# Context stage of a perceiver layer: two products written as 64-column halves, and another order of transfers on SyncE

## The chip, the core and the metric

The kernel runs on one core of a Trainium2 chip. The metric is the device time of one execution in microseconds (us), as the median of several. All data are f32 unless said otherwise.

## What is computed

The reference adds three blocks to x (64 sequences of 64 tokens, 256 features). Only the first concerns this change:

```python
v = jnp.einsum('bsd,hd->bsh', visual_features, Wv) + bv     # of layernorm(x), 64 tokens per sequence
t = jnp.einsum('bsd,hd->bsh', text_features, Wt) + bt       # of ctx_768, 256 rows of 192 features per sequence
dots = jnp.einsum('bih,bjh->bij', v, t)
vn, tn = jnp.linalg.norm(v, axis=-1), jnp.linalg.norm(t, axis=-1)
return dots / jnp.maximum(vn[:, :, None] * tn[:, None, :], EPS)   # added to x
```

The second block is a self-attention with 16 heads, the third a mixture of 14 experts of which each token takes one.

## The kernel before

There are three stages: context (the block above), attention, experts. The context stage goes through 16 pairs of sequences (NB = 16; one pair is 128 tokens twice, that is two tiles of tokens). All engines run the same list of pairs, each with an order written out by hand, and wait for each other on counting semaphores. TensorE's step for pair i holds, in this order:

- t's first pass (lines 1303 and 1306): 128 of the 192 context features, two products with 512 moving columns each, into two PSUM banks (`t_bank(p, 0)` and `t_bank(p, 1)`). The stationary operand is `wt_s`, 128 columns wide.
- the values v (line 1324, from the fifth pair on; the first four, `TURNED = 4`, use line 1327 on turned tiles): two products with 256 moving columns, stationary `wvc_s`, 128 columns wide, moving `xT_s`.
- t's second pass (line 1352): the other 64 features, two products on 64 rows of the array each.
- for the pair before: v's squared norms (line 1293), t's squared norms (line 1363, two products on 64 columns of the array), and the dots (line 1367, four products on 64 columns, 256 moving columns each).

The step for the 15th pair also holds some small products for the router (lines 1376, 1341, 1344), the one for the 16th a transposition for attention (line 1282).

What follows for a pair: VectorE multiplies norms (line 724), ScalarE takes logarithm and exponential (1103, 1105), VectorE makes the cosines (755), GpSimd adds them to the tokens (528), VectorE takes statistics of the sum (709, 714). TensorE's line 1293 of the next pair waits for the cosines of this one (`cos_sbuf`). From the fifth pair on v is made of raw x: VectorE (line 696) adds the bias times each token's standard deviation to it, and for that it needs the deviations along the free axis on all partitions. They are made by GpSimd (`deviation`, lines 491 to 498, six pairs ahead, after its line 528), written to memory by SyncE (line 356) and read back as 128 copies into `std_b` (line 365, `spread_deviations`). After line 696 ScalarE squares v (1115) and evacuates t (1125, 1126) before it comes to line 1103 again.

SyncE asks for nearly all transfers from one queue, in order; a wait there holds up everything behind it. Its step i (`load_tokens`) waits for t's second pass of pair i-4, then asks for xT and the context of pair i (lines 344, 345; four buffers), spreads the deviations of pair i-2, asks for x of pair i+3 (i+2 in the first steps), and writes the deviations of pair i (`deviations`), for which it waits for GpSimd. In steps 8 to 13 two constants each follow. `std_b` has two buffers.

On GpSimd, VectorE, ScalarE and TensorE some of the middle steps stand in a hardware loop of four steps per turn (`run_steps`), which makes one turn (two on ScalarE).

Of the kernel before, what the change touches and what calls it, by code (L numbers as in the profile page):

```python
# [15 lines left out]
P = 128  # L16
B, S, D = 64, 64, 256
SC, DC, H = 256, 192, 128
# [5 lines left out]
NB = NT // 2  # L24
# [19 lines left out]
TURNED = 4  # L44
AHEAD = 6
LO, HI = 8, 28
RING, RLO, RHI = 8, 12, 28
# [78 lines left out]
def build(nc, x, xT, ctxT, wvT, wtT, xb, wqT, wkT, avT, woT, bq, bk, bv, bo, boc, woN, routerT, w1, w2, b1T, b2, out):  # L126
# [3 lines left out]
    with ctx:  # L130
# [3 lines left out]
        def sem(name):  # L134
            return ctx.enter_context(nc.semaphore(name))
# [58 lines left out]
        vT, vsq = (arena[:, 4096 + n * 2 * D:4096 + (n + 1) * 2 * D].rearrange("p (s j) -> p s j", s=2) for n in range(2))  # L194
        std_b = arena[:, 2048:2048 + 4 * P].rearrange("p (s j) -> p s j", s=2)
        wvc_s = arena[:, 2048 + 4 * P:2048 + 4 * P + KC * H].rearrange("p (c h) -> p c h", c=KC)
        pair_rstd, pair_rvar, pair_std = (arena[:, 3072 + n * NT:3072 + (n + 1) * NT] for n in range(3))
# [100 lines left out]
        ctx_in = [sem(f"ctx_in{n}") for n in range(4)]  # L298
        std_in = [sem(f"std_in{n}") for n in range(2)]
        std_out = [sem(f"std_out{n}") for n in range(2)]  # L300
        rec_out = [sem(f"rec_out{n}") for n in range(RING)]
# [23 lines left out]
        def _(sp):  # L325
# [9 lines left out]
            def load_tokens(i, k):  # L335
# [5 lines left out]
                else:  # L341
                    need(sp, s["t_psum"], i - 3)
                    if not isinstance(i, int) or i >= TURNED:
                        sp.dma_start(xT_s[:, k], xT[bass.ds(i, 1)].rearrange("o p j -> (o p) j")).then_inc(ctx_in[k], 16)
                    sp.dma_start(ctx_in_sb[:, k], ctxT[bass.ds(i, 1)].rearrange("o p j -> (o p) j"))\
                        .then_inc(ctx_in[k], 16)
                def turned(n):
                    return isinstance(n, int) and not TURNED <= n < NB
                if not turned(i - 2):
                    spread_deviations(i - 2, k % 2)  # L350
                for n in (i + 2,) if i < 4 else (i + 2, i + 3) if i == 4 else (i + 3,):
                    if n < NB:
                        load_x(n, n % 4)
                if not turned(i):
                    need(sp, s["a_std"], i - TURNED + 1)
                    sp.dma_start(deviations[bass.ds(i, 1)].rearrange("o p h -> (o p) h"), pair_std[:, bass.ds(i * 2, 2)])\
                        .then_inc(std_out[k % 2], 16)
                if 8 <= i < 8 + RESTS // 2:
                    for to, source in rest[2 * (i - 8):2 * (i - 7)]:
                        sp.dma_start(to, source).then_inc(s["consts_in"], 16)  # L360

            def spread_deviations(n, q):
                need(sp, std_out[q], arrivals(n - TURNED, q, 2, 16))
                need(sp, s["v_sbuf"], n - 1)
# [4 lines left out]
            for n in (NB - 2, NB - 1):  # L369
                spread_deviations(n, n % 2)  # L370

# [66 lines left out]
        def _(pool):  # L438
# [97 lines left out]
            def attention_step(i, k):  # L536
# [49 lines left out]
                return send  # L586
            run_steps(pool, context_step, -4, NB - 1, 6, 10)
            pool.wait_ge(s["consts_in"], 16 * RESTS)
# [47 lines left out]
        def _(dve):  # L636
# [13 lines left out]
            def context_step(j, k):  # L650
# [39 lines left out]
                if paired(v) and not (isinstance(v, int) and v < TURNED):  # L690
                    need(dve, s["v_psum"], v + 1)
                    need(dve, s["dots_psum"], v - 1)
                    need(dve, std_in[p], arrivals(v - TURNED, p, 2, 16))
                    if isinstance(v, int) and v == TURNED:
                        dve.wait_ge(s["first_made"], 6)
                    dve.scalar_tensor_tensor(vT[:, p, :].rearrange("f (h t) -> f h t", h=2),
                                             std_b[:, p, :].rearrange("f (t h) -> f h t", h=2), xbs_s[:, :],
                                             bank(p, 2 * P).rearrange("f (h t) -> f h t", h=2), ALU.mult, ALU.add)\
                        .then_inc(s["v_sbuf"], 1)
# [61 lines left out]
            def attention_step(i, k, parts=("tile", "ranked", "lcs", "sums", "late"), aside=()):  # L761
# [145 lines left out]
                if live(u):  # L907
                    need(dve, s["smax_ok"], u + 1)
                    need(dve, s["pT_psum"], u - 1)
                    if isinstance(u, int) and u == 0:  # L910
# [3 lines left out]
                        .then_inc(s["centred"], 1)  # L914
            run_steps(dve, context_step, -4, NB - 3, 6, 10)
            attention_step(-1, 3)
# [172 lines left out]
        def _(act):  # L1089
# [71 lines left out]
            def attention_step(i, k):  # L1161
# [39 lines left out]
                if live(u):  # L1201
                    spread_second_values((k - 1) % 2, (k - 1) % 4)
            run_steps(act, context_step, -1, NB, 4, 12)
            context_step(NB, NB)
# [66 lines left out]
        def _(pe):  # L1271
# [13 lines left out]
            def context_step(i, k):  # L1285
# [10 lines left out]
                if paired(t):  # L1296
# [5 lines left out]
                    need(pe, s["t_sbuf"], t - 1)  # L1302
                    pe.matmul(t_bank(p, 0), wt_s[:, 0, :], ctx_in_sb[:, k, 0:2 * SC], start=True, stop=False)
                    if isinstance(i, int) and i == 0:
                        pe.wait_ge(ctx_in[0], 16)
                    pe.matmul(t_bank(p, 1), wt_s[:, 0, :], ctx_in_sb[:, k, 2 * SC:4 * SC], start=True, stop=False)
                    if isinstance(i, int) and i == 0:
# [119 lines left out]
            def attention_step(i, k):  # L1427
# [84 lines left out]
            run_steps(pe, context_step, -1, NB, 8, 12)  # L1512
            pe.wait_ge(s["consts_made"], CONSTS)
# [164 lines left out]
```

## Time and profile before

| | us |
|---|---|
| median of 3 runs | 495.55 |
| lowest and highest run | 494.43, 496.55 |
| profiled execution | 494.51 |
| its span, first to last instruction | 492.7 |
| TensorE busy | 479.8 (97% of the span) |
| VectorE, ScalarE, GpSimd busy | 335.6, 331.6, 243.9 |

The profiled execution spends 1.81 us outside its span. The context stage fills the time to about 104 us, attention the next 235 us or so, the experts the rest; they overlap a little. Matmuls are pipelined, so their rows overlap: the time a product takes is read from one start to the next. An f32 product makes two MATMUL records, hence "x2" for one product, "x4" for two.

### The profile page before, as it was taken

The numbers are of one execution on the slowest core, as the hardware profiler recorded it, in microseconds if no ns is written. First come the engines' busy times: TensorE is split into PE (matmuls) and PEld (weight loads), VectorE is DVE, ScalarE is ACT, GpSimd is POOL, SyncE is SP. The second block draws the span as 40 slices with busy tenths as digits, with TensorE's granted clock in tenths as the row PEclk, the third lists the DMA queues.
The fourth block names the chain that finished last, engine by engine and source line by source line (L and its number), as shares of the span: only waits on it lengthen the run. The fifth ranks groups of instructions, "written<-read, shape, count | busy, mean of one in ns | idle before, by whom it ended". The sixth has DMA issues, their size and how long they took to land.

```text
span 492.7 us, 13958 instructions
## 1 busy us (share of the span) xinstructions
PE 479.8 (97%) x4290; PEld 384.0 (78%) x4291; DVE 335.6 (68%) x1021; ACT 331.6 (67%) x804; POOL 243.9 (50%) x428
## 2 busy tenths in 40 slices
PE   8999999999999999999999999998999999999996
PEld 6544444567888888888888888877898999999995
DVE  3577665657788989999898999998573333333332
ACT  2765666569988998898898889886553334333432
POOL 3468764344444456474655657472555333233333
PEclk9999999999999999999999999999999999999999
DMA  8989997500001223313322221227465876675631
GB/s 305 284 195 298 297 311 207 177 2 2 1 2 39 51 88 98 98 61 87 100 57 91 67 59 51 67 84 227 152 220 160 266 229 203 207 232 192 193 131 37
DMA packets 35025, 69.32 MB, mean 141 GB/s; under 512 B 6592, under 2 KB 21826, under 8 KB 34960
## 3 DMA queue, kind: packets, MB, share of 16 engines
q1 hardware_dynamic: 31168, 59.40, 40.3%
q0 software_dynamic: 3360, 8.84, 4.8%
q8 instruction: 34, 0.56, 0.5%
q10 hardware_dynamic: 432, 0.26, 0.2%
q14 instruction: 31, 0.25, 0.2%
HBM read 57.61 MB, written 11.35 MB: 140 GB/s over the span
## 4 chain that ended last, share of the span: by engine, by line
PE 65%; DVE 6%; issue 4%; ACT 3%; POOL 2%; POOLq 0%; ACTq 0%; DVEq 0%
PE psum L1532 13%; PE psum L1545 12%; PE psum L1459 9%; PE psum L1436 6%; PE psum L1423 6%; PE psum L1415 6%; PE psum L1383 5%; PE psum L1488 5%; PE psum L1282 5%; DVE arena L912 1%; POOL tok L528 1%; POOL out L614 1%; ACT arena L1145 0%; DVE smax L901 0%; ACT arena L1181 0%
## 5 line engine op out<-in xcount | busy, mean ns | idle before, releaser
L1532 PEld LDWEIGHTS psum<-arena,ring 128*128 128x128 f32 x608 | 73.5, 192 | 2.6 <-issue 0.6
L1532 PE MATMUL psum<-arena,ring 128*128 128x128 f32 x608 | 74.1, 275 | 0.5 <-issue 0.5
L1545 PE MATMUL psum<-w_s,arena 128*128 x304 | 71.9, 380 | 0.0
L1215 ACT ACTIVATE arena<-psum 128x256 f32<-128x256 f32 x38 | 14.6, 385 | 81.7 <-PE psum L1282 74.8
L1036 DVE SCALAR_TENSOR_TENSOR arena<-psum,slot_rec,arena 128x256 f32<-128x256 f32 x38 | 18.4, 484 | 69.3 <-PE psum L1545 69.0
L556 POOL TENSOR_TENSOR ov<-o_n,v_s 128x256 f32<-128x256 f32 x32 | 26.1, 817 | 77.8 <-DVE o_n L794 77.8
L1545 PEld LDWEIGHTS psum<-w_s,arena 128*128 128x128 f32 x304 | 55.0, 190 | 6.1
L1181 ACT ACTIVATE arena<-kT,head_mask 128x256 f32<-128x256 f32 x128 | 59.3, 531 | 0.0
L614 POOL DMA_INDIRECT out<-arena,token_of x38 | 38.8, 1022 | 19.0 <-POOL token_of L606 14.1
L901 DVE TENSOR_REDUCE smax<-psum 128x16 f32<-128x1024 f32 x32 | 39.2, 1224 | 12.6 <-PE psum L1436 12.6
L1145 ACT ACTIVATE arena<-arena 128x1024 f32<-128x1024 f32 x32 | 33.8, 1057 | 19.0 <-DVE arena L912 18.9
L1221 ACT ACTIVATE arena<-psum,b_s 128x128 f32<-128x128 f32 x152 | 43.3, 375 | 3.5 <-PE psum L1532 2.2
L552 POOL DMA_INDIRECT routed<-rec,pos x32 | 33.5, 1047 | 15.0 <-issue 6.5
L1415 PEld LDWEIGHTS psum<-arena 128*64 128x64 f32 x1024 | 32.4, 138 | 9.5 <-issue 8.3
L912 DVE TENSOR_TENSOR arena<-psum,smax 128x1024 f32<-128x1024 f32 x32 | 37.9, 1183 | 0.0
L606 POOL TENSOR_TENSOR token_of<-slot_rec,zero_u 128x1 uint32<-128x1 uint32 x38 | 9.1, 239 | 58.1 <-DVE arena L1036 58.0
L1436 PE MATMUL psum<-arena,qT 64*64 64x256 f32 x512 | 35.0, 389 | 1.6 <-DVE arena L912 1.6
L1415 PE MATMUL psum<-arena 128*64 128x34 f32 x1024 | 36.1, 225 | 0.4 <-ACT arena L1131 0.3
L1488 PE MATMUL psum<-av_s,xnT 128*128 128x270 f32 x128 | 34.7, 393 | 1.2 <-DVE logit L813 1.1
L1423 PE MATMUL psum<-wo_s,oT 128*128 128x270 f32 x128 | 35.2, 397 | 0.3 <-ACT oT L1141 0.3
L1459 PEld LDWEIGHTS psum<-xnT,wq_s 128*128 128x128 f32 x256 | 33.2, 191 | 2.2
L1459 PE MATMUL psum<-xnT,wk_s 128*128 128x128 f32 x256 | 34.2, 276 | 0.7 <-issue 0.7
(206 smaller groups left out, 1072.9 us busy)
## 6 DMA issues: line engine op xcount, KB each, us to landing
ring<-w SPq DMA_DIRECT2D x38, 512.0 KB
w_s<-ctxT SPq DMA_DIRECT2D x15, 768.0 KB, 8.5
w_s<-w SPq DMA_DIRECT2D x16, 448.0 KB, 3.4
slot_rec<-routed SPq DMA_DIRECT2D x38, 132.0 KB
tok<-x SPq DMA_DIRECT2D x16, 256.0 KB, 7.8
w_s<-xT SPq DMA_DIRECT2D x12, 256.0 KB, 6.8
routed<-pad_rec SPq DMA_DIRECT2D x1, 1980.0 KB, 8.6
tok<-b SPq DMA_DIRECT2D x14, 128.0 KB, 3.1
```

Of the source, the lines that this page charges most:

```text
L614: pool.indirect_dma_start(out=out, out_offset=bass.IndirectOffsetOnAxis(ap=token_of[:, q, :], axis=0), in_=yout[:, q, :], in_offset=None, ...
L901: dve.tensor_reduce(smax[:, :], s_ps, AX.X, ALU.max).then_inc(s["smax_ok"], 1)
L912: dve.tensor_tensor(prob[:, (k - 1) % 2, :].rearrange("p (h j) -> p h j", h=NH), s_ps, smax[:, :].unsqueeze(2).broadcast_to([P, NH, S]), A ...
L1181: last = act.activation(kd[:, p, :, :, g * S:(g + 1) * S], kT[:, p, :].rearrange("p (c b j) -> p c b j", c=KC, b=2), ACT.Copy, scale=head_ ...
L1221: last = act.activation(hidT[:, p, f * P:(f + 1) * P], hid_bank(p)[:, f * P:(f + 1) * P], ACT.Gelu, bias=b1_s[:, bass.ds(e * FC + f, 1)])
L1415: mm = pe.matmul(bank(7)[h, n * VW:(n + 1) * VW], probT[:, p, n * P + b * S:n * P + (b + 1) * S], vd[:, p, b, n, :], start=True, stop=True)
L1423: mm = pe.matmul(bank(6, DX), oT[:, q, d * P:(d + 1) * P], wo_s[:, d, :], start=d == 0, stop=d == KC - 1)
L1436: mm = pe.matmul(bank(g)[h, c * HG * S:(c + 1) * HG * S], qT[r, q, c * P + b * S:c * P + (b + 1) * S], kd[r, q, c, b, :], start=True, stop ...
L1459: mm = pe.matmul(bank(4)[:, at:at + P], weight[:, d, c * P:(c + 1) * P], xnT[:, p, d * P:(d + 1) * P], start=d == 0, stop=d == KC - 1)
L1488: mm = pe.matmul(bank(6, DX), xnT[:, p, d * P:(d + 1) * P], av_s[:, d, :], start=d == 0, stop=d == KC - 1)
L1532: mm = pe.matmul(hid_bank(p)[:, f * P:(f + 1) * P], w1_s[:, r, c * F + f * P:c * F + (f + 1) * P], xgT[:, p, c * P:(c + 1) * P], start=c = ...
L1545: mm = pe.matmul(bank(2 + q, D), hidT[:, q, f * P:(f + 1) * P], w2_s[:, bass.ds(e * (FC * D) + f * D, D)], start=f == 0, stop=f == FC - 1)
```

## The change

- t's first pass and the values are issued, from the fifth pair on, as two products each, one for either half of 64 output columns (64 PSUM partitions); the moving operand is the same for both.
- `std_b` has four buffers (`SPREAD = 4`) in place of two, with semaphores to match; `wvc_s` moves in the arena.
- SyncE asks for x before it spreads deviations, and from the sixth step for x of pair i+4 instead of i+3. From the ninth step it spreads pair i-1 instead of i-2, and writes the deviations of pair i+1 instead of i; the ninth step does two of each.
- The hardware loops of the context stage on the four engines are written out.

```diff
-        std_b = arena[:, 2048:2048 + 4 * P].rearrange("p (s j) -> p s j", s=2)
-        wvc_s = arena[:, 2048 + 4 * P:2048 + 4 * P + KC * H].rearrange("p (c h) -> p c h", c=KC)
+        std_b = arena[:, 2048:2048 + 8 * P].rearrange("p (s j) -> p s j", s=SPREAD)
+        wvc_s = arena[:, 3328:3328 + KC * H].rearrange("p (c h) -> p c h", c=KC)
...
-                def turned(n):
-                    return isinstance(n, int) and not TURNED <= n < NB
-                if not turned(i - 2):
-                    spread_deviations(i - 2, k % 2)
-                for n in (i + 2,) if i < 4 else (i + 2, i + 3) if i == 4 else (i + 3,):
+                for n in (i + 2,) if i < 4 else (i + 2, i + 3) if i == 4 else (i + 3, i + 4) if i == 5 else (i + 4,):
                     if n < NB:
                         load_x(n, n % 4)
-                if not turned(i):
-                    need(sp, s["a_std"], i - TURNED + 1)
-                    sp.dma_start(deviations[bass.ds(i, 1)].rearrange("o p h -> (o p) h"), pair_std[:, bass.ds(i * 2, 2)])\
-                        .then_inc(std_out[k % 2], 16)
+                first = TURNED + 4
+                if i >= TURNED + 2:
+                    for n in (i - 2,) if i < first else (i - 2, i - 1) if i == first else (i - 1,):
+                        spread_deviations(n)
+                if i >= TURNED:
+                    for n in (i,) if i < first else (i, i + 1) if i == first else (i + 1,):
+                        if n < NB:
+                            write_deviations(n)
...
-            def spread_deviations(n, q):
-                need(sp, std_out[q], arrivals(n - TURNED, q, 2, 16))
-                need(sp, s["v_sbuf"], n - 1)
+            def write_deviations(n):
+                sp.wait_ge(s["a_std"], n - TURNED + 1)
...
+            def spread_deviations(n):
+                q = n % SPREAD
+                sp.wait_ge(std_out[q], arrivals(n - TURNED, q, SPREAD, 16))
+                need(sp, s["v_sbuf"], n - SPREAD + 1)
...
-            run_steps(pool, context_step, -4, NB - 1, 6, 10)
+            lay_steps(context_step, -4, NB - 1)
...
-                    pe.matmul(t_bank(p, 0), wt_s[:, 0, :], ctx_in_sb[:, k, 0:2 * SC], start=True, stop=False)
+                    halved = not (isinstance(t, int) and t < TURNED)
+                    def first_pass(b):
+                        moving = ctx_in_sb[:, k, b * 2 * SC:(b + 1) * 2 * SC]
+                        if not halved:
+                            pe.matmul(t_bank(p, b), wt_s[:, 0, :], moving, start=True, stop=False)
+                            return
+                        for h in (slice(0, RG), slice(RG, P)):
+                            pe.matmul(t_bank(p, b)[h, :], wt_s[:, 0, h], moving, start=True, stop=False)
+                    first_pass(0)
...
-                            mm = pe.matmul(bank(p, 2 * P), wvc_s[:, c, :], xT_s[:, k, c * 2 * P:(c + 1) * 2 * P],
-                                           start=c == 0, stop=c == KC - 1)
+                            for h in (slice(0, RG), slice(RG, P)):
+                                mm = pe.matmul(bank(p, 2 * P)[h, :], wvc_s[:, c, h], xT_s[:, k, c * 2 * P:(c + 1) * 2 * P],
+                                               start=c == 0, stop=c == KC - 1)
```

## Rows read from the trace of the kernel before

**Rows 1.** Pairs five to sixteen: busy us of PE, PEld, DVE, ACT, POOL; clock; DMA.
```profile
30.80:101.70 70.90, 70.90 (x378) 33.93 (x376) 46.41 (x163) 42.31 (x59) 44.46 (x116) 1.00 0.83 230
```
**Rows 2.** Timeline of TensorE, step of the 13th pair: start, duration, line, operands.
```profile
78.14 1.12 PE L1303 MATMUL psum<-w_s,wt_s 128*128 128x512 f32 x2
79.11 1.02 PE L1306 MATMUL psum<-w_s,wt_s 128*128 128x512 f32 x2
79.97 1.03 PE L1324 MATMUL psum<-w_s,arena 128*128 128x256 f32 x4
80.92 1.13 PE L1352 MATMUL psum<-w_s,wt_s 64*128 64x512 f32 x4
81.98 0.40 PE L1293 MATMUL psum<-ones,arena 128*64 128x1 f32 x8
82.24 1.06 PE L1363 MATMUL psum<-w_s,ones 128*64 128x512 f32 x4
83.12 1.03 PE L1367 MATMUL psum<-w_s,arena 128*64 128x256 f32 x8
84.09 1.13 PE L1303 MATMUL psum<-w_s,wt_s 128*128 128x512 f32 x2
```
**Rows 3.** Group of weight loads for the dots (busy, mean ns, idle before).
```profile
L1367 PEld LDWEIGHTS psum<-w_s,arena 128*64 128x64 f32 x128 | 9.3, 137 | 11.3 <-issue 9.1
```
**Rows 4.** Timeline of TensorE, step of the 15th pair.
```profile
90.03 0.62 PE L1376 MATMUL psum<-rt_s,ones 128*128 128x14 f32 x4
93.16 0.96 PE L1341 MATMUL psum<-av_s,woN_s 128*128 128x14 f32 x8
```
**Rows 5.** Timeline of VectorE, ScalarE, GpSimd: one turn of the cosines, a later line 696.
```profile
66.27 0.20 POOL L498 TENSOR_TENSOR arena<-pair_vareps,arena 128x2 f32<-128x2 f32 x1
66.38 0.88 DVE L724 TENSOR_SCALAR arena<-psum,vnorm 128x256 f32<-128x256 f32 x2 [0.28 <-PE psum L1367]
67.29 0.63 ACT L1103 ACTIVATE arena<-arena 128x512 f32<-128x512 f32 x1 [0.82 <-DVE arena L724]
68.61 0.87 DVE L755 SCALAR_TENSOR_TENSOR arena<-arena,psum 128x256 f32<-128x256 f32 x2 [0.42 <-ACT arena L1105]
69.57 1.27 POOL L528 TENSOR_TENSOR tok<-tok,arena 128x512 f32<-128x512 f32 x1 [1.89 <-DVE arena L755]
70.87 0.75 DVE L709 BATCH_NORM_STATS2 stats<-tok 128x6 f32<-128x256 f32 x2 [0.99 <-POOL tok L528]
71.83 0.12 DVE L704 TENSOR_TENSOR vnorm<-psum,arena 128x2 f32<-128x2 f32 x1
87.23 0.47 DVE L696 SCALAR_TENSOR_TENSOR arena<-arena,xbs_s,psum 128x256 f32<-128x256 f32 x1
```
**Rows 6.** Timeline of the same engines, sixth pair, and TensorE's line 1293 behind it.
```profile
40.67 0.48 DVE L696 SCALAR_TENSOR_TENSOR arena<-arena,xbs_s,psum 128x256 f32<-128x256 f32 x1 [0.82 <-DMA arena<-deviations]
42.51 1.11 ACT L1126 ACTIVATE w_s<-psum,xb_s 128x1024 f32<-128x1024 f32 x1
42.54 0.12 DVE L704 TENSOR_TENSOR vnorm<-psum,arena 128x2 f32<-128x2 f32 x1
42.81 0.88 DVE L724 TENSOR_SCALAR arena<-psum,vnorm 128x256 f32<-128x256 f32 x2
45.04 0.87 DVE L755 SCALAR_TENSOR_TENSOR arena<-arena,psum 128x256 f32<-128x256 f32 x2 [0.42 <-ACT arena L1105]
46.33 0.40 PE L1293 MATMUL psum<-ones,arena 128*64 128x1 f32 x8
```
**Rows 7.** DMA, 36 to 40 us, in all.
```profile
DMA packets 689, 1.32 MB, mean 331 GB/s; under 512 B 121, under 2 KB 475, under 8 KB 688
```
**Rows 8.** From request to landing: deviations spread (line 365), written (356), context (345).
```profile
DMA to landing us min/median/max: 3.0/8.0/10.8
DMA to landing us min/median/max: 3.6/9.1/10.6
DMA to landing us min/median/max: 6.2/8.5/11.1
```

More of the change, by code:

```diff
@@ L45 @@
 AHEAD = 6
+SPREAD = 4
 LO, HI = 8, 28
@@ L298, in build @@
         ctx_in = [sem(f"ctx_in{n}") for n in range(4)]
-        std_in = [sem(f"std_in{n}") for n in range(2)]
-        std_out = [sem(f"std_out{n}") for n in range(2)]
+        std_in = [sem(f"std_in{n}") for n in range(SPREAD)]
+        std_out = [sem(f"std_out{n}") for n in range(SPREAD)]
         rec_out = [sem(f"rec_out{n}") for n in range(RING)]
@@ L360, in load_tokens @@
                         sp.dma_start(to, source).then_inc(s["consts_in"], 16)
-            def spread_deviations(n, q):
-                need(sp, std_out[q], arrivals(n - TURNED, q, 2, 16))
-                need(sp, s["v_sbuf"], n - 1)
+            def write_deviations(n):
+                sp.wait_ge(s["a_std"], n - TURNED + 1)
+                sp.dma_start(deviations[bass.ds(n, 1)].rearrange("o p h -> (o p) h"), pair_std[:, bass.ds(n * 2, 2)])\
+                    .then_inc(std_out[n % SPREAD], 16)
+            def spread_deviations(n):
+                q = n % SPREAD
+                sp.wait_ge(std_out[q], arrivals(n - TURNED, q, SPREAD, 16))
+                need(sp, s["v_sbuf"], n - SPREAD + 1)
                 sp.dma_start(std_b[:, q, :], deviations[bass.ds(n, 1)].rearrange("o p h -> o (p h)").broadcast_to([P, 2 * P]))\
@@ L368, in _ @@
                 load_tokens(i, i % 4)
-            for n in (NB - 2, NB - 1):
-                spread_deviations(n, n % 2)
+            spread_deviations(NB - 1)
             sp.wait_ge(s["consts_made"], CONSTS)
@@ L692, in context_step @@
                     need(dve, s["dots_psum"], v - 1)
-                    need(dve, std_in[p], arrivals(v - TURNED, p, 2, 16))
+                    r = (k + 1) % SPREAD
+                    need(dve, std_in[r], arrivals(v - TURNED, r, SPREAD, 16))
                     if isinstance(v, int) and v == TURNED:
@@ L696, in context_step @@
                     dve.scalar_tensor_tensor(vT[:, p, :].rearrange("f (h t) -> f h t", h=2),
-                                             std_b[:, p, :].rearrange("f (t h) -> f h t", h=2), xbs_s[:, :],
+                                             std_b[:, r, :].rearrange("f (t h) -> f h t", h=2), xbs_s[:, :],
                                              bank(p, 2 * P).rearrange("f (h t) -> f h t", h=2), ALU.mult, ALU.add)\
@@ L914, in attention_step @@
                         .then_inc(s["centred"], 1)
-            run_steps(dve, context_step, -4, NB - 3, 6, 10)
+            lay_steps(context_step, -4, NB - 3)
             attention_step(-1, 3)
@@ L1202, in attention_step @@
                     spread_second_values((k - 1) % 2, (k - 1) % 4)
-            run_steps(act, context_step, -1, NB, 4, 12)
+            lay_steps(context_step, -1, NB)
             context_step(NB, NB)
@@ L1302, in context_step @@
                     need(pe, s["t_sbuf"], t - 1)
-                    pe.matmul(t_bank(p, 0), wt_s[:, 0, :], ctx_in_sb[:, k, 0:2 * SC], start=True, stop=False)
+                    halved = not (isinstance(t, int) and t < TURNED)
[7 more added lines that the diff above has]
+                    first_pass(0)
                     if isinstance(i, int) and i == 0:
                         pe.wait_ge(ctx_in[0], 16)
-                    pe.matmul(t_bank(p, 1), wt_s[:, 0, :], ctx_in_sb[:, k, 2 * SC:4 * SC], start=True, stop=False)
+                    first_pass(1)
                     if isinstance(i, int) and i == 0:
@@ L1511, in attention_step @@
                     turn_output(y, (k - 3) % 2)
-            run_steps(pe, context_step, -1, NB, 8, 12)
+            lay_steps(context_step, -1, NB)
             pe.wait_ge(s["consts_made"], CONSTS)
```

## Prediction

> **What bounds the kernel now.** I read the busy time by stage first. From the fifth to the sixteenth pair, the steps that the change touches, TensorE is busy 70.90 of 70.90 us at the full granted clock (2.4 GHz); the next engine has 46.41 [rows 1]. So nothing waits there but the others for TensorE, and a gain must come out of TensorE's own list of work. I then read one step of that list from start to start [rows 2]: t's first pass takes 0.97 and 0.86 us, the values 0.95, t's second pass 1.06, v's norms 0.26, t's norms 0.88, the dots 0.97: 5.95 us for a pair. The two products of the first pass are alike, yet the first takes 0.11 more; it stands behind products on 64-column halves, the second behind its own kind. The dots, just ahead of it, are four products of 256 columns, two at a time, and should take what one product of 512 takes (0.86); they take 0.97, another 0.11. So the passage from half columns to full columns costs 0.22 us. t's norms show that two halves do run side by side: two products of 512 moving columns on 64 columns each take 0.88, where one on all 128 takes 0.86.
>
> Next I looked for what stands close behind TensorE. One turn of the cosines on the other engines [rows 5]: line 724 to 1103 takes 0.91, to 755 1.32, to GpSimd's 528 0.96, to 709 1.30, to 704 0.96, and from 704 to the next 724 0.27 at the least [rows 6]: 5.72 us. Before, this ring has 0.23 us of slack per pair.
>
> **The change part by part.** *Halves.* With t's first pass and the values on halves, nothing changes form from the norms of a pair to the values of the next. Removed per pair: 0.22 us. The halves themselves I cost at nothing: four instead of two products at two at a time, as the norms and dots show [rows 2]. The passage from the values to t's second pass is 0.09 in the values and some part of the 0.20 that the second pass takes over 0.86; whether it is dearer or cheaper coming from halves no row shows. I bound it by that passage free (0.1 less) and doubled (0.1 more), and take no change, as the passages shown cost alike: over 12 pairs 1.2 us either way. The two halves also read the same moving columns, which no row shows; if that kept them from running side by side it is the third rival.
>
> Pair by pair: the fifth step follows single-column norms (halves too) and gains 0.11, the sixth to fourteenth 0.22 each (nine). In the 15th step the router's small products, all on full columns, come between [rows 4]: before, only the passage into line 1376 costs; after it there are also one back to halves and one into line 1341, so the step loses 2 x 0.22 = 0.44. In the 16th a transposition on full columns stands behind the values: one passage less, one more, 0. If TensorE never waits the sum is 0.11 + 9 x 0.22 - 0.44 = 1.65 us.
>
> *The ring of the cosines.* The new pace is 5.95 - 0.22 = 5.73 us, the ring's 5.72. So it can just follow, but it cannot win back a delay, and line 1293 will wait for every one. One shows already. In the sixth pair VectorE waits 0.82 us for the spread deviations; that puts ScalarE's line 1126 at 42.51 and the cosines' end at 45.04 + 0.87 = 45.91, with line 1293, in TensorE's seventh step, at 46.33 [rows 6]. After the change TensorE would be there 0.11 + 2 x 0.22 = 0.55 sooner, at 45.78, but the cosines are ready at about 46.0 (a release takes about 0.1: 755's end at 69.48 to 528's start at 69.57 [rows 5]).
>
> *SyncE: x ahead.* No transfer of x is waited for in this stretch, since TensorE never waits [rows 1], so x a pair sooner gains nothing by itself. But in SyncE's eighth step the spread of the sixth pair's deviations now stands behind x of a pair (256 KB). What runs at that moment moves 331 GB/s [rows 7], so it lands 0.79 us later. As a bound from below it costs nothing (if the queue isn't full yet); I take 0.79, as that spread took 8 us, the median, like one in a filled queue [rows 8]. Then line 696 starts at 41.46, ScalarE's 1126 1.84 later (42.51 - 40.67) at 43.30, ends at 44.40, 1103 follows at once, 755 1.32 later at 45.72, ends at 46.59, and line 1293 comes at 46.69: 0.36 later than before, 0.91 later than it could.
>
> *SyncE: deviations.* From the ninth step each spread is asked for a pair (5.7 us) sooner, so the waits of line 696 that later pairs have (up to 0.8 us) should go; TensorE's slack hid them before, and without slack they would cost that much each. The writing hardly gets sooner: the write waits for GpSimd's line 498, which comes where it did. So SyncE, now writing one pair further ahead, stands in that wait at the end of each step, with xT and context of the next step behind it. Line 498 for the 14th pair ends at 66.47 [rows 5]; the step behind it could start when line 1293 does, three steps of 5.95 before 81.98 [rows 2], at 64.13: it starts 2.3 us late, and two constants later. The context is asked for three steps (17.2 us) before its use and lands after 11.1 at most [rows 8], so 6.1 us are to spare: cost nothing. If that cover went, TensorE would wait for the rest.
>
> *Four buffers, loops written out.* The spread no longer waits for line 696 two pairs back, which comes sooner than it is needed: nothing. The loops' turns show no gap on TensorE [rows 1], and idle time of the others is covered by it: nothing.
>
> *Sum.* In the seventh step 0.36 later; then seven steps at 5.73 against 5.95, eighth to fourteenth, 7 x 0.22 = 1.54 sooner; 0.44 back in the 15th: 0.74 us sooner at the stage's end. The ring has 0.01 us to spare per pair; 0.05 more in each of seven turns would take 0.35, which I keep for the range. Attention and experts are TensorE's as well (97% of the span), so the gain is passed on. Of the profiled execution, 494.51 with 1.81 outside its span, that leaves 493.77. That execution lies 1.04 below the median of the runs, 495.55; off the median I get 494.8.
>
> **The rivals.** *No wait at the sixth pair* (the spread isn't later, or VectorE takes it up): the whole 1.65, so 493.9; with the passage to the second pass cheaper by its bound another 1.2, 492.7. For it: the queue was drained before that spread. Against it: the ring alone, with the old landing, is 0.2 late.
>
> *Deviations late all the way*, the one that ends slower. Between GpSimd's line 498 for a pair (66.47) and the line 696 that needs it (87.23) lie 20.8 us before [rows 5], some 20.0 at the new pace. Writing and spreading take 9.1 + 8.0 = 17.1 at the median and 10.6 + 10.8 = 21.4 at the most [rows 8]; the second is asked for only when the first has landed, and I put 0.6 for the requests ahead of it, a guess. From 20.0 on line 696 waits, then ScalarE, the cosines, TensorE, and GpSimd's next deviations with them: a ring over five pairs. At the most it is 22.0, then 4.4 from line 696 to the cosines (45.04 - 40.67 [rows 6]), and 3.8 from these to the next line 498's end (66.47 less 68.61 - 5.95 [rows 5]): 30.2 against 5 x 5.73 = 28.65, 1.5 us late in each turn, and there are two until the 16th pair: 3.1 us, 0.74 off, so 2.4 later than before, 497.9. Against it: the spreads come a pair sooner in the queue.
>
> *The halves do not hide.* One after the other, the first pass and the values take 2.6 us more per pair [rows 2], twelve pairs 31 us: 526. Against it stand t's norms and the dots.
>
> *The halves' weight loads show.* Each half loads 64 columns; 16 loads a pair at 137 ns [rows 3], one by one, are 2.2 us, 26 in all: 521. Against it: the dots' eight loads have that form, 1.1 us together, and lie inside 0.97 us without a gap [rows 2]. The Trainium skill ("TensorE: Matmul & The Clock Gate", section "Part 3: Packing small matmuls — row/col tiling") says that a weight load runs beside a matmul only where their row groups differ, and both halves use all rows. The dots' rows disagree with it.
>
> *The change of form isn't what costs* (the 0.22 belongs to the order of banks or operands): then nothing is removed, and the wait in the seventh step, 0.36, is all that changes: 495.9.
>
> **How the numbers follow.** Forecast (0.74 sooner, 494.8): 0.52. No wait: 0.22. Nothing removed: 0.10. Deviations late: 0.12. Halves not hidden: 0.03. Weight loads: 0.01. A measurement of this kernel tells 0.5% (2.5 us) from no change, so the forecast counts as the same, as do nothing removed and most of no wait. Faster by more needs the cheap passage and no wait, or a gain on the ramp into attention that I don't see: 0.15. Slower: late deviations about as they are priced there, and halves: 0.12. The range: below 1.65 + 1.2, with a median's scatter of about 0.6, 492.1; above, the passage dearer (+1.2), the ring (+0.35) and the late deviations, 498.0.
>
> **What would show it.** In the changed trace: lines 1367 to the first pass 0.86 apart, first pass to values 0.86 and 0.86, step 5.73. A wait on TensorE before line 1293 in the seventh step, put down to VectorE's cosines, of up to 0.9 us. Line 696 waiting for deviations in the sixth pair and not in the twelfth and thirteenth. SyncE's wait at the writes longer. I am wrong if the step is 5.95 still, if waits before 1293 recur in each pair, or if the end moves by other than the start of attention does.

## The result and the profile after

The changed kernel takes 497.63 us (median of 7 runs, 496.88 to 498.47) against 495.55 before: a ratio of 1.004, interval 1.002 to 1.0059. It is 0.4% slower, where 0.74 us less was forecast. In a second batch it took 498.67 against 496.21: 1.0047, interval 1.0026 to 1.0068.

In code after the change, t's first pass is line 1317, the values 1340, the second pass 1368, v's norms 1300, t's norms 1379, the dots 1383. Here is the step of the 13th pair on TensorE (timeline: start, duration, line), to lay beside [rows 2]:

```profile
78.55 1.03 PE L1383 MATMUL psum<-w_s,arena 128*64 128x256 f32 x8
79.42 1.89 PE L1317 MATMUL psum<-w_s,wt_s 128*64 128x512 f32 x8
81.13 1.03 PE L1340 MATMUL psum<-w_s,arena 128*64 128x256 f32 x8
82.10 1.13 PE L1368 MATMUL psum<-w_s,wt_s 64*128 64x512 f32 x4
83.16 0.34 PE L1300 MATMUL psum<-ones,arena 128*64 128x1 f32 x5
```

The dots now take 0.87 (were 0.97) and the first pass 1.71 (1.83); values 0.97 (0.95) and second pass 1.06 (1.06) stay. The halves do what they were meant to. From the seventh to the 14th step TensorE never stops (its row by windows: length, busy time of PE, PEld, DVE, ACT, POOL, then clock, DMA share, GB/s):

```profile
48.69:88.90 40.21, 40.21 (x280) 17.58 (x281) 27.05 (x91) 25.85 (x35) 25.93 (x72) 1.00 0.98 263
```

Seven steps in 40.21 us are 5.74 each, where before they took 5.94. The loss is ahead of them, in the seventh step (TensorE; in brackets the idle time before and what ended it):

```profile
40.02 0.40 PE L1300 MATMUL psum<-ones,arena 128*64 128x1 f32 x8
45.03 1.08 PE L1340 MATMUL psum<-w_s,arena 128*64 128x256 f32 x8 [1.12 <-DVE vnorm L711]
46.04 1.13 PE L1368 MATMUL psum<-w_s,wt_s 64*128 64x512 f32 x4
48.69 0.40 PE L1300 MATMUL psum<-ones,arena 128*64 128x1 f32 x8 [1.51 <-issue]
```

V's norms come at 48.69, before at 46.33 [rows 6]: 2.36 later. The reader follows the two waits back on VectorE and ScalarE (line 703 is the old 696, 1133 the old 1126, 762 the old 755):

```profile
43.51 0.48 DVE L703 SCALAR_TENSOR_TENSOR arena<-arena,xbs_s,psum 128x256 f32<-128x256 f32 x1 [3.90 <-DMA arena<-deviations]
45.40 1.10 ACT L1133 ACTIVATE w_s<-psum,xb_s 128x1024 f32<-128x1024 f32 x1
47.71 0.87 DVE L762 SCALAR_TENSOR_TENSOR arena<-arena,psum 128x256 f32<-128x256 f32 x2 [0.79 <-ACT arena L1112]
```

VectorE stands 3.90 us at line 703, for the sixth pair's spread deviations; all behind it follows as it must. On SyncE's queue x stands ahead of that spread, and the eighth pair's write stands behind it (timeline). The second view has the requests of x and of the spread by their lines (request at, then from request to landing):

```profile
33.59 0.75 SPq L365 DMA_DIRECT2D deviations<-arena  x1
```

```profile
L333 SPq DMA_DIRECT2D tok<-x x1: 432/432/432, 32.6 to 32.6; - x1
...
DMA to landing us min/median/max: 7.3/7.3/7.3
...
L372 SPq DMA_DIRECT2D arena<-deviations x1: 411/411/411, 33.1 to 33.1; - x1
...
DMA to landing us min/median/max: 10.2/10.2/10.2
```

In the kernel before the same two requests stand the other way round, the spread first (32.69) and x behind it, next to the write. The same view of that kernel, spread first:

```profile
L365 SPq DMA_DIRECT2D arena<-deviations x1: 376/376/376, 32.7 to 32.7; - x1
...
DMA to landing us min/median/max: 7.9/7.9/7.9
...
L332 SPq DMA_DIRECT2D tok<-x x1: 432/432/432, 33.1 to 33.1; - x1
...
DMA to landing us min/median/max: 10.4/10.4/10.4
```

So in these two executions it is the place next to the write that takes over 10 us, whoever stands in it. Before, x did, which nobody waited for.

I measure the context stage from v's norms of the first pair to attention's first product, as the start scatters by up to 1.5 us from one execution to the next. Before:

```profile
11.97 0.40 PE L1293 MATMUL psum<-ones,arena 128*64 128x1 f32 x8
...
103.82 0.38 PE L1459 MATMUL psum<-xnT,wk_s 128*128 128x128 f32 x1
```

and after:

```profile
11.95 0.40 PE L1300 MATMUL psum<-ones,arena 128*64 128x1 f32 x8
...
105.00 0.49 PE L1475 MATMUL psum<-xnT,wk_s 128*128 128x128 f32 x2
```

91.85 and 93.05 us: 1.20 longer. The profiled executions differ by 4.0 us of span, though. A second step is at 334 us: TensorE's granted clock is 0.89 on average from 330 to 345 us, where it is 1.00 in the kernel before; from 335 to 337 us it is 0.50, the lower of its two levels (1.2 GHz), and line 1452 takes 1.99 us at 334.87 (the same line took 1.09 before). It stands behind 1.56 us without work for TensorE, as it does before (1.57). The rest comes after GpSimd's last request, which it makes at 489.69 before (line 614) and at 492.13 after (line 620). These are 2.44 apart; the spans end 3.0 and 4.6 us later. A second profile of the changed kernel, below, has neither of the two.

### The profile page after: what moved, and what is told of

The parts are those of the page before. It is cut to its first block, busy times and chain, and to the rows that moved or that the text cites. A ratio compares the mean times of both kernels' runs of the same rounds, so it can differ in the third digit from the quotient of the medians.

```text
span 496.7 us, 14132 instructions
## 1 busy us (share of the span) xinstructions
PE 480.4 (97%) x4386; PEld 382.2 (77%) x4387; DVE 335.2 (67%) x1021; ACT 331.3 (67%) x804; POOL 243.9 (49%) x428
## 4 chain that ended last, share of the span: by engine, by line
PE 66%; DVE 5%; issue 4%; ACT 2%; POOL 2%; ACTq 0%; POOLq 0%; DVEq 0%
PE psum L1548 13%; PE psum L1561 12%; PE psum L1475 9%; PE psum L1452 6%; PE psum L1439 6%; PE psum L1431 6%; PE psum L1289 5%; PE psum L1504 5%; PE psum L1399 5%; DVE arena L919 1%; POOL tok L534 1%; POOL out L620 1%; ACT arena L1152 0%; DVE smax L908 0%; ACT arena L1188 0%
```

## The experiments

"Context" is the stage as measured above, in one profiled execution; "landing" the sixth pair's spread from request to landing; "wait" VectorE's for it. A pair in brackets is another one for whose spread VectorE waited over 0.3 us. Ratios are to the kernel before on the same chip, with their interval.

| kernel | landing | wait | other waits | context | ratio |
|---|---|---|---|---|---|
| before | 7.9 | 0.82 | 0.38 (12th), 0.81 (13th) | 91.85 | |
| after | 10.2 | 3.90 | | 93.05 | 1.004 (1.002 to 1.0059) |
| after_again | 10.5 | 4.01 | 0.78 (5th), 0.52 (13th) | 93.29 | 1.0047 (1.0026 to 1.0068) |
| halves_only | 6.9 | 0 | | 90.40 | 0.9972 (0.9949 to 0.9995) |
| moves_only | 10.2 | 3.74 | | 94.22 | 1.0025 (1.0001 to 1.0048) |
| loops_only | 7.4 | 0.39 | 0.60 (11th), 1.45 (12th) | 91.92 | 0.9988 (0.9966 to 1.001) |
| spread_first | 7.2 | 0.38 | | 90.25 | 0.9942 (0.9918 to 0.9966) |
| spread_first_again | 7.6 | 0.73 | 0.54 (11th), 0.34 (12th), 2.40 (13th) | 91.79 | 0.9971 (0.995 to 0.9991) |
| eighth_step | 7.3 | 0 | 2.10 (5th) | 91.26 | 0.9992 (0.9968 to 1.0016) |
| spread_first_14 | 7.4 | 0.55 | 0.71 (10th), 0.74 (11th), 1.83 (12th) | 91.20 | 0.9985 (0.9964 to 1.0005) |
| write_later | 7.5 | 0.97 | 0.84 (5th), 0.51, 1.71, 1.44 (9th to 11th) | 92.03 | one execution |
| write_two_rows | 7.9 | 1.51 | | 90.67 | one execution |
| write_by_act | 10.8 | 4.26 | 0.84 (5th) | 93.61 | 1.0044 (1.002 to 1.0067) |
| write_by_act_first | 7.4 | 0.62 | 1.69 (7th) | 91.03 | 0.9983 (0.9964 to 1.0001) |
| two_rows_all | 6.5 | 0 | | 90.24 | 0.9975 (0.9955 to 0.9996) |
| sixteen_rows_all | 6.8 | 0.47 | | 90.24 | 0.996 (0.9938 to 0.9982) |

**The parts alone.** First the halves without the rest:

```diff
 kernel before
-                    pe.matmul(t_bank(p, 0), wt_s[:, 0, :], ctx_in_sb[:, k, 0:2 * SC], start=True, stop=False)
+                    first_pass(0)      # in halves, as in the change; the values likewise
```

> The kernel before with t's first pass and the values on 64-column halves, and nothing else of the change. Theory (the halves gain, SyncE's new order at its eighth step loses): the spread deviations of the sixth pair land where they did, about 40.6 us; line 1300 (v's norms) of TensorE's seventh step about 46.3 as before, a step of 5.75 after it, attention's first product about 1.2 us before 103.82, so 102.6; median 494.3. Rival (the halves themselves lose, because the ring of the cosines cannot follow at 5.75): waits of TensorE in every pair, attention at 103.8 or later, median 495.5 or more. If the deviations of later pairs bind without the sooner requests, VectorE's line for t's values waits in several pairs and attention comes between, about 103.2.

Measured: 494.61 us, 0.9972, context 90.40, 1.45 shorter than before. V's norms and the start of attention:

```profile
46.23 0.40 PE L1293 MATMUL psum<-ones,arena 128*64 128x1 f32 x8
...
102.60 1.16 PE L1468 MATMUL psum<-xnT,wk_s 128*128 128x128 f32 x8
```

The seventh step takes 5.96 (40.27 to 46.23), 0.2 over the pace. That is the ring: line 755 makes the cosines from 45.26 to 46.13, and line 1293 follows at 46.23, as late as the prediction had it for the old landing. All later steps up to the 14th take 5.74 to 5.79. So from there the ring of the cosines follows. Then the rest without the halves:

```diff
 changed kernel
-                    first_pass(0)      # and first_pass(1), and the values, on all 128 columns again
+                    pe.matmul(t_bank(p, 0), wt_s[:, 0, :], ctx_in_sb[:, k, 0:2 * SC], start=True, stop=False)
```

> The changed kernel with t's first pass and the values back on full columns: SyncE's new order, the four buffers and the loops written out remain. Theory (SyncE's order loses): the spread of the sixth pair lands about 43.4 us, VectorE waits some 3.5 us for it, TensorE's seventh step is 2 to 2.4 us late at v's norms, and with steps of 5.95 nothing is won back: attention's first product at 105.8 to 106.2 against 103.82, median 497.6 to 498. Rival (the halves lose): attention at 103.8, median 495.5.

Measured: 498.03 us, 1.0025; landing 10.2, context 94.22, 2.37 longer than before. The two parts add up to 0.92, the whole change gives 1.20 and 1.44. And the loops:

```diff
 kernel before, on all four engines
-            run_steps(pe, context_step, -1, NB, 8, 12)
+            lay_steps(context_step, -1, NB)
```

> The kernel before with the four engines' context loops written out and nothing else. Theory (a written-out loop costs nothing, TensorE's list is the same): attention's first product at 103.8, median 495.5, within 0.3. Rival (the program's length costs, in code fetched or in the place where the granted clock falls): a dip of the granted clock before the experts or a later end, 0.7 us or more above before.

Measured: 495.88 us, 0.9988 with 1 inside the interval, context 91.92. Writing the loops out costs nothing that shows.

**The place in SyncE's queue.** One line changes places:

```diff
 changed kernel, load_tokens
-                for n in (i + 2,) if i < 4 else ...: load_x
                 if i >= TURNED + 2: spread_deviations
+                for n in (i + 2,) if i < 4 else ...: load_x
```

> The changed kernel with one thing back: in each of SyncE's steps the spread of the deviations is asked for ahead of x again, x still a pair sooner. Theory (the place behind x at SyncE's eighth step is what makes the spread of the sixth pair late): it lands about 40.6 us, line 1300 of the seventh step at 46.3, attention's first product about 102.6, that is 2.4 sooner than with the change and 1.2 sooner than before; median 494.3. Rival (x a pair sooner loads the queue, in whatever order): the spread lands 42 us or later, attention at 104.5 to 105, median 497.

Measured: 492.98 us, 0.9942; landing 7.2, context 90.25. X a pair sooner does no harm; its place ahead of the spread does. The ratio is better than the context explains (1.60 of 496); so I ran it again:

> The kernel with the spread ahead of x in every step, halves everywhere, once more beside the others: context stage 90 to 91.5 us; the median 1.5 to 3 us under before. If the earlier 0.994 was a lucky batch, the ratio comes out at 0.996 to 0.999.

Measured: 495.26 us against 496.21, 0.9971. The first ratio was partly luck, but the kernel is faster than the one before in both batches, and so than the changed one. Its context took 91.79 in this execution, 1.5 longer than the first time, all of it in one wait of VectorE for the 13th pair's spread:

```profile
82.88 0.48 DVE L703 SCALAR_TENSOR_TENSOR arena<-arena,xbs_s,psum 128x256 f32<-128x256 f32 x1 [2.40 <-DMA arena<-deviations]
```

Next the spread ahead of x in the eighth step alone (`if i != 7` ahead of x's place in the change, `if i == 7` behind the spread):

> The changed kernel with the spread ahead of x in SyncE's eighth step alone; in all other steps x stays ahead. Theory (the whole loss is this one place): line 703 of the sixth pair at about 41 us instead of 43.5, v's norms of the seventh step 5.9 us after those of the sixth instead of 8.7, no other wait of TensorE, and from v's norms of the first pair to attention's first product 90.3 us as with the spread first everywhere (93.05 with the change); median 493 to 494.5. Rival (other steps' spreads are late as well, hidden so far by the delay): a wait at line 703 in the fifth or a later pair, and 91 us or more.

Measured: 496.23 us, 0.9992. The sixth pair's spread lands in 7.3, as the theory has it. But in this execution VectorE waited 2.10 us for the fifth pair's, which still stood behind x; in the two profiles of the change it had been 0.30 and 0.78. Against the first of them its request came 0.93 us later (26.16 for 24.52, each counted from v's norms of the first pair), and it took 10.3 to land instead of 9.5, with the next write asked for (32.00) while it was in flight. So the loss is not in one place only, and the rival was half right.

**What the write does.** I moved the eighth pair's write:

```diff
 changed kernel, load_tokens
+                    if i == 8:
+                        write_deviations(7)      # behind xT and context of the ninth step
...
-                if i >= TURNED:
+                if i >= TURNED and i != 7:
```

> The changed kernel, x still ahead of the spread at SyncE's eighth step, but the write of the eighth pair's deviations, asked for right behind that spread, is moved behind xT and context of the next step, about 2 us later. Theory A (a write of deviations holds up the transfer that stands directly ahead of it in the queue): the spread of the sixth pair lands with the x ahead of it, line 703 of the sixth pair at about 40.5 us, v's norms of the seventh step 5.9 us after the sixth's. The next pairs' deviations come later then, by up to 2 us, so line 703 may wait in the eighth pair. Theory B (the bytes of x, or a stall that comes at about 41 us whatever stands there): line 703 at 42 us or later, seventh step 7.5 us or more.

Measured (one execution, 496.05 us): landing 7.5, wait 0.97, seventh step 5.92. The spread by its line:

```profile
L374 SPq DMA_DIRECT2D arena<-deviations x1: 411/411/411, 33.1 to 33.1; - x1
...
DMA to landing us min/median/max: 7.5/7.5/7.5
```

With x and its bytes still ahead of it, the spread is in time when the write isn't next to it: theory A. I had expected that the eighth pair might then wait; it is the 9th to 11th that do. Then I changed the write's shape:

```diff
 changed kernel, write_deviations
+                if n == 7:
+                    sp.dma_start(deviations[bass.ds(n, 1)].rearrange("o (a p) h -> (o a) (p h)", a=2), ones[0:2, :])...
+                    return
```

> The changed kernel in its own order, but the eighth pair's deviations are written as two rows of 512 bytes (of ones, so this pair's values are not its own) instead of 128 rows of 8 bytes. Theory A1 (the 128 small rows hold up the spread ahead of them): line 703 of the sixth pair at 40.5 us, seventh step 5.9 us. Theory A2 (any write to memory there does it): part of the engines late still, line 703 at 42 us or more. Theory B (nothing to do with the write): as with the change, 43.5 us.

Measured (one execution, 493.45 us): landing 7.9, against 8.0 for x ahead of it in the queue. VectorE waits 1.51 all the same, since x itself landed at 40.85, after 39.91 in the first profile of the change; the spread lies 0.4 us behind x instead of 3.4. Seventh step 6.28: between A1 and A2 by the numbers I had put, but the landings speak for A1. Then another queue:

```diff
 changed kernel, load_tokens
-                        if n < NB:
+                        if n < TURNED + 3:
                             write_deviations(n)
...
 changed kernel, context_step on ScalarE, ahead of its square of v
+                if TURNED <= t < NB - 3:
+                    act.wait_ge(s["a_std"], t - TURNED + 4)
+                    act.dma_start(deviations[bass.ds(t + 3, 1)]..., pair_std[:, bass.ds(2 * (t + 3), 2)])...
```

> The changed kernel with x still ahead of the spreads; the deviations of the eighth and later pairs are written by ScalarE (in front of its square of v, where it waits 1.4 us now), so that no write stands behind the sixth pair's spread in SyncE's queue and SyncE no longer waits for GpSimd. Theory Q (the write holds up what stands ahead of it in its own queue): that spread lands 7.5 us after its request, line 703 of the sixth pair at about 40.5 us, no wait for deviations later, context stage 90.3 to 90.8 us. Theory E (the write holds up the DMA engines, from whatever queue it comes): the spread or other transfers in flight at that moment are late by 2 to 3 us all the same, line 703 at 42 us or more, context stage 91.5 to 93. Rival (ScalarE's requests lengthen the ring of the cosines): waits of TensorE at v's norms in every pair.

Measured: 498.34 us, 1.0044. ScalarE's write, x and the spread, by their lines:

```profile
L1115 ACTq DMA_DIRECT2D deviations<-arena x1: 347/347/347, 32.8 to 32.8; - x1
...
DMA to landing us min/median/max: 11.0/11.0/11.0
...
L333 SPq DMA_DIRECT2D tok<-x x1: 434/434/434, 32.7 to 32.7; - x1
...
DMA to landing us min/median/max: 11.0/11.0/11.0
...
L372 SPq DMA_DIRECT2D arena<-deviations x1: 412/412/412, 33.2 to 33.2; - x1
...
DMA to landing us min/median/max: 10.8/10.8/10.8
```

Theory E, and the context of 93.61 is even longer than I had put for it (91.5 to 93). The write on an otherwise empty queue takes as long as on SyncE's, and now x, next to it in time, is late too (11.0 instead of 7.3 and 8.7 in the two profiles of the change). The Trainium skill ("DMA: Bandwidth & Descriptors", section "Issuing engines are not separate DMA queues") says that transfers run on the same 16 DMA engines whichever engine starts them; these three rows agree. ScalarE's requests themselves cost no step: seven steps from 49.32 to 89.53, 5.74 each.

Finally the shape in all pairs, first two rows, then sixteen. Both kernels write ones in place of the deviations, so their values are not the layer's; only their times are read:

```diff
 changed kernel, write_deviations
-                sp.dma_start(deviations[bass.ds(n, 1)].rearrange("o p h -> (o p) h"), pair_std[:, bass.ds(n * 2, 2)])\
+                sp.dma_start(deviations[bass.ds(n, 1)].rearrange("o (a p) h -> (o a) (p h)", a=2), ones[0:2, :])\
```

Sixteen rows are the same with `a=16` and `ones[0:16, 0:16]`.

> The changed kernel in its own order, x ahead of every spread, with all pairs' deviations written as two rows of 512 bytes (of ones: the scale of t's values is not the tokens' own) instead of 128 rows of 8 bytes. Theory R (the many small rows of a write are what makes transfers in flight late, in every pair): the spread of the sixth pair lands 7.5 to 8 us after its request, no wait of line 703 above 0.7 in the fifth to sixteenth pair, no wait of TensorE from the fifth step on, context stage 90.2 to 90.5 us in place of 93.1 to 93.3; median 1.5 to 3 us under before. Rival S (the bytes of x and the order of the queue are enough): the sixth pair's spread at 8.7 us or more, TensorE waits in the seventh step, context stage 91 or more. Rival T (any write, of whatever rows): 93.

> As with two rows in every pair, but sixteen rows of 64 bytes (of ones again): the bytes of a write are the same, and so is the order of the queue. Theory N (the number of rows counts): as with two rows, the sixth pair's spread 6.5 to 8 us after its request, no wait of line 703 above 0.7, context stage 90.2 to 90.6 us. Theory W (writes of small rows spread over many DMA engines count, whatever their number): the spread at 9 us or more, TensorE waits in the seventh step, context stage 92 or more.

Measured: 494.57 us, 0.9975, and 493.38 us, 0.996; context 90.24 in both, and no wait of TensorE after the first pairs, with x ahead of every spread. From 30 to 80 us the requests' median time to landing (last number), in the changed kernel:

```profile
w_s<-ctxT SPq DMA_DIRECT2D x8, 768.0 KB, 9.4
tok<-x SPq DMA_DIRECT2D x5, 256.0 KB, 9.1
arena<-deviations SPq DMA_DIRECT2D x9, 128.0 KB, 9.3
deviations<-arena SPq DMA_DIRECT2D x10, 1.0 KB, 7.7
```

and with sixteen rows:

```profile
w_s<-ctxT SPq DMA_DIRECT2D x9, 768.0 KB, 6.7
tok<-x SPq DMA_DIRECT2D x5, 256.0 KB, 5.0
arena<-deviations SPq DMA_DIRECT2D x10, 128.0 KB, 6.7
deviations<-ones SPq DMA_DIRECT2D x10, 1.0 KB, 3.8
```

The same bytes in the same order land 2.6 to 4.1 us sooner. So the shape of the write is the cause: 1 KB in 128 rows of 8 bytes holds the others up, in 16 rows of 64 bytes it doesn't. Rival W, as I had put it, is out. That it is the number of rows (theory N) isn't shown: with the number their size changed too, from 8 to 64 bytes, and the source of the write. Nor do 128 rows of 8 bytes take long in every direction: `bq_s`, 1 KB read from memory in 128 such rows, lands 1.8 us after its request in sixteen_rows_all. What is shown holds for the write to memory.

**The rest of the difference.** The changed kernel as it is, beside the others:

> The changed kernel once more, profiled and timed beside the others. The context stage (v's norms of the first pair to attention's first product) took 93.05 us with the change and 91.85 before: 1.2 of the 2.1 us by which the medians differ. Theory (the rest is scatter that every kernel has: the granted clock falls in one place in some executions, and the spreads' landings differ): context stage 92.5 to 94, spread of the sixth pair again 9 to 10.5 us from request to landing; median 1.2 to 2 above the median of before. Rival (the change costs something behind the context stage): from attention's first product to the end 1 us or more above the 388.9 of before without a fall of the granted clock.

Measured: 498.67 against 496.21 us, 2.46 above where I had put 1.2 to 2. The profiled execution is one with the full clock (windows view, 330 to 345 us; the columns as above):

```profile
330.00:345.00 15.00, 13.25 (x163) 10.70 (x162) 13.03 (x38) 10.76 (x23) 5.30 (x9) 1.00 0.74 232
```

and its row in the first profile of the change:

```profile
330.00:345.00 15.00, 13.27 (x152) 10.00 (x151) 11.59 (x35) 9.33 (x21) 4.45 (x9) 0.89 0.73 225
```

Context 93.29, and from attention's first product to the end of the span 493.9 - 105.28 = 388.6, where the kernel before has 492.7 - 103.82 = 388.9. So in this execution the change costs nothing behind the context stage. It is the fastest of its twelve, though (495.71), so it doesn't show what the median one loses there. The medians differ by 2.1 and 2.5 us, the contexts by 1.2 and 1.4. Part of the rest goes with the clock: in this batch the mean granted clock over the span is 0.9956 on average of the 12 runs of the change and 0.9982 of the 35 of before. Over 496 us the difference is 1.3 us, an estimate. The fall at 334 us shows in 6 of 16 profiles (after, moves_only, eighth_step, write_later and two with the spread first). Whether waits of TensorE in the context stage make it likelier stays open: moves_only loses most there, and its runs have 0.9982 too.

**Two attempts at a better kernel.** Full columns in the 15th step, on top of the spread first:

```diff
+                    halved = not (isinstance(t, int) and (t < TURNED or t == NB - 2))
```

> The spread ahead of x in every step, and in TensorE's 15th step first pass and values on full columns, as before. The 15th step took 7.88 us from v's norms to v's norms with halves there and 7.64 before. Theory (the router's products on full columns make the halves cost more passages than they save in that step): 7.64 again, from v's norms of the first pair to attention's first product 90.0 us against 90.25; median 492.8, about the same as with halves there. Rival (the passage back to halves only moves to the 16th step): 90.25 or more.

Measured: 495.65 us, 0.9985. The 15th step takes 7.63 us as expected (7.88 with halves), but in this execution the 10th to 12th pairs' spreads are late, TensorE waits 1.1 us, and the context is 91.20. With ScalarE's writes in addition (both diffs together):

> The best of what the runs point to: halves, each spread ahead of x, ScalarE writing the deviations from the eighth pair on, full columns in the 15th step. Context stage 90.0 us (90.25 with the spread first and halves everywhere); no wait of line 703 beyond 0.5. If the landings' scatter is what spreads the run times, the median lies at or under that of the spread-first kernel and the runs lie closer. If ScalarE's requests cost, 91 or more.

Measured: 495.47 us, 0.9983, context 91.03 with one wait of 1.69 for the seventh pair's spread. The spread, asked for 0.11 us ahead of ScalarE's write, lands in 7.4 here, and x behind it in 10.8; so not each request beside the write is late. No gain over the spread first; late spreads stay in both runs. With the write in two or sixteen rows there is none above 0.47, in one profile each. Both runs show that a single execution's landing differs by more than what the 15th step can give.

## Why the prediction was wrong, point by point

- **TensorE bounds the stage, and the passage between half and full columns costs 0.22.** Held: 0.20 per pair came out. The halves hide, their weight loads too, and the unknown passage from the values to the second pass costs what it did before (values 0.97, second pass 1.06). The three rivals on halves are out. The rule of the Trainium skill on weight loads that I had weighed ("TensorE: Matmul & The Clock Gate", "Part 3: Packing small matmuls — row/col tiling") doesn't hold here: first pass and values make 16 loads a pair in place of 8, and the step is shorter.
- **Fifth and sixth step, 0.33 together.** Measured 0.34 (30.54 to 40.02 after, 30.56 to 40.38 before).
- **The seventh step, 0.36 later: the step that failed.** My chain from line 696 to line 1293 was 5.23 us long, measured are 5.18. What was wrong is its start: 41.46 by the sum, 43.51 in fact. I had priced the place behind x by x's bytes over the queue's rate, 0.79 us, and zero as the other end. In fact line 703 came 2.84 later than its counterpart before (43.51 for 40.67): the request came 0.45 later (33.14 for 32.69), and the landing moved from 7.9 to 10.2 us (10.5 in the second profile). The price stood in the trace before: the request that was then next to the write, x, took 10.4. A spread that takes over that place takes over its time. My rows for landings [rows 8] have a maximum of 10.8 for the spread, so an upper end for that landing was there too; I used that number only in a rival.
- **Seven steps at 0.22: 1.54.** Measured 46.33 to 87.92 before and 48.69 to 88.90 after: 1.38.
- **The 15th step loses 0.44.** It loses 0.24. Three rows of the step before, to lay beside [rows 4], and the step after:

```profile
90.50 1.10 PE L1303 MATMUL psum<-w_s,wt_s 128*128 128x512 f32 x2
...
92.30 1.03 PE L1324 MATMUL psum<-w_s,arena 128*128 128x256 f32 x4
...
93.97 0.60 PE L1344 MATMUL psum<-bor_s,ones 128*128 128x14 f32 x4
```

```profile
90.04 1.03 PE L1383 MATMUL psum<-w_s,arena 128*64 128x256 f32 x8
91.01 0.62 PE L1392 MATMUL psum<-rt_s,ones 128*128 128x14 f32 x4
91.55 1.94 PE L1317 MATMUL psum<-w_s,wt_s 128*64 128x512 f32 x8
93.32 1.03 PE L1340 MATMUL psum<-w_s,arena 128*64 128x256 f32 x8
94.28 1.06 PE L1357 MATMUL psum<-av_s,woN_s 128*128 128x14 f32 x8
95.20 0.60 PE L1360 MATMUL psum<-bor_s,ones 128*128 128x14 f32 x4
```

  From half to full columns costs what I had sized: the values take 0.96 (0.86 before) and line 1357 0.92 (0.81), 0.21 together. The way back is nearly free: line 1392 takes 0.54 to the first pass (0.47), and the first pass 1.77 (1.80). I had booked 0.22 for that way too.
- **The sum.** 2.36 - 1.38 + 0.24 - 0.04 (16th step) = 1.18 later at attention, where I had 0.36 - 1.54 + 0.44 = 0.74 sooner. Between the two lie 1.92: 2.00 more in the seventh step, 0.16 less won in the seven, 0.20 less lost in the 15th, 0.04 won in the 16th.
- **SyncE's other moves cost nothing.** Held: SyncE waits longer at the writes (18.7 us in all up to attention, 11.9 before), it also waits 15.9 us for writes to land before it spreads them (2.4 before), and TensorE never waits for the context. The loops cost nothing that shows.
- **Deviations late all the way.** Not in the change: VectorE doesn't wait for them after the sixth pair in the first profile, and in the second once, 0.52 for the 13th, at no cost to TensorE. Single spreads of later pairs are late in some executions of other orders (by 2.40 us in spread_first_again, where TensorE then waits 1.5, and by 1.45 in loops_only, whose 5.95 us a pair leave 0.08 of it). At 5.75 no slack is left to take it.
- **"The end moves by other than the start of attention does"** I had named as a sign of being wrong. It did in the first profile (the clock, the end) and not in the second. The cause of the later end, 4.6 instead of 3.0 us behind GpSimd's last request, stays open.
- **"A measurement tells 0.5% from no change."** It told 0.4% here, with an interval of 1.002 to 1.0059.

## What to carry to other kernels

Price a new place in a queue by the request that stood there before, from its own request to its landing, and look at what stands next to it; bytes over bandwidth is only the lowest price. When an engine's slack is spent, look for what scatters behind it: here a gain of 1.45 us was shown by the halves alone, and one landing of 10 instead of 8 us took it back and more. And a write of 1 KB to memory isn't small when it is 128 rows of 8 bytes: look at the rows, not only at the bytes.

## What the runs showed of the hardware

- A write of 128 rows of 8 bytes to memory holds up what is in flight with it on the DMA engines: in SyncE's eighth step the neighbour lands 9.1 to 11.0 us after its request, and x or the spread with no such write beside it in 6.9 to 8.7; it does so from SyncE's queue and from ScalarE's. With 16 rows of 64 bytes x lands in 5.0 at the median instead of 9.1. So a DMA share of 0.98 at 263 GB/s (in the window above) didn't mean that the bytes needed the time: with sixteen rows the same seven steps have 0.85 at 288 GB/s.
- The Trainium skill ("DMA: Bandwidth & Descriptors", section "Specifications") gives 512 bytes as the smallest transfer at full rate. Rows of 8 and of 64 bytes both lie below it, and here those of 64 did no harm that shows, so that limit alone doesn't tell the two apart; whether the number of rows or their size does stays open.
- The granted clock fell to its lower level (0.50, 1.2 GHz) at 334 to 337 us in 6 of 16 profiled executions and not in the others. In all 16 of them TensorE stands without work for 1.56 or 1.57 us there.
